# A recommendation tower on one core: wide triple products, a last chunk contracted by units, GpSimd with gathers only

## The reference: what is computed

```python
x_i = einsum('bmd,bhd->bmhd', X, prev_x).reshape(b, m * h, d)
x_i = einsum('oc,bcd->bod', W, x_i) + b[None, :, None]     # 128 outputs
cin_outs.append(x_i.sum(axis=2))                            # summed over d
```

## Time and profile before

| | us |
|---|---|
| three runs | 258.37, 261.34, 262.34 |
| median | 261.34 |
| the profiled execution | 258.26 |
| its span, first to last instruction | 256.5 |
| busy: TensorE / weight loads / VectorE | 209.3 / 173.8 / 127.2 |
| busy: ScalarE / GpSimd | 84.4 / 148.8 |
| mean granted TensorE clock (1 is full speed) | 0.939 |
| product matmuls L212, 4,096 records | 63.7 |
| contraction matmuls L371, 616 records | 76.9 |

### The profile page before, as it was taken

How to read it: one execution, slowest core, us unless ns; L and a number is a source line. 1 busy time by engine, 2 the same in 40 slices (tenths; PEclk the granted TensorE clock), 3 DMA queues, 4 the chain that set the end, 5 groups by cost and what they waited for, 6 DMA issues and landing times.

```text
span 256.5 us, 10809 instructions
## 1 busy us (share of the span) xinstructions
PE 209.3 (82%) x5049; PEld 173.8 (68%) x5049; DVE 127.2 (50%) x194; ACT 84.4 (33%) x159; POOL 148.8 (58%) x142
## 2 busy tenths in 40 slices
PE   7897899499007889799898796979698896999995
PEld 6664667287006769688787584968697796899541
DVE  0559487666920866838649548173918641000000
ACT  2575447264202961413433313142313310100141
POOL 4778788877899778778778778777750000000000
PEclk9999799979856999999999999799889997999999
DMA  6811111112810111111111111111110000000000
GB/s 206 299 26 20 31 28 23 24 33 35 279 22 3 23 26 25 30 23 31 30 24 30 27 24 31 20 32 28 29 26 3 5 3 5 0 3 0 0 0 0
DMA packets 6564, 9.66 MB, mean 38 GB/s; under 512 B 2804, under 2 KB 3256, under 8 KB 6520
## 3 DMA queue, kind: packets, MB, share of 16 engines
q0 software_dynamic: 4096, 4.20, 9.1%
q1 hardware_dynamic: 2136, 4.19, 4.7%
q10 hardware_dynamic: 288, 0.59, 0.7%
HBM read 8.97 MB, written 0.00 MB: 35 GB/s over the span
## 4 chain that ended last, share of the span: by engine, by line
POOL 43%; PE 36%; issue 15%; DMA 3%; ACT 2%; DVE 0%; DVEq 0%; ACTq 0%; POOLq 0%
POOL rows L413 39%; PE psum L371 19%; PE psum L212 7%; PE psum L491 3%; PE psum L482 3%; DMA rows<-table,idx 2%; POOL t_sb L306 2%; POOL prod L261 2%; PE psum L280 1%; PE psum L193 1%; PE psum L286 1%; ACT t_sb L229 1%; DMA t_sb<-ids 1%; PE psum L474 0%; ACT prod L250 0%
## 5 line engine op out<-in xcount | busy, mean ns | idle before, releaser
L413 POOL DMA_INDIRECT rows<-table,idx x128 | 138.8, 1085 | 40.6 <-issue 38.1
L212 PE MATMUL psum<-prod,xx 64*32 64x77 f32 x4096 | 63.7, 243 | 23.7 <-POOL prod L261 13.4
L261 DVE TENSOR_TENSOR prod<-xx 128x1024 f32<-128x1024 f32 x62 | 73.7, 1220 | 6.8 <-ACT xx L241 4.0
L212 PEld LDWEIGHTS psum<-prod,xx 64*32 64x32 f32 x4096 | 51.4, 109 | 35.9 <-issue 16.2
L371 PE MATMUL psum<-t_sb,coef 128*128 128x128 f32 x552 | 67.9, 285 | 2.1 <-issue 2.1
L371 PEld LDWEIGHTS psum<-t_sb,coef 128*128 128x128 f32 x552 | 66.7, 202 | 2.4 <-issue 2.2
L229 ACT ACTIVATE t_sb<-psum 128x616 f32<-128x616 f32 x34 | 23.3, 685 | 79.8 <-PE psum L212 79.8
L226 DVE COPY t_sb<-psum 128x616 f32<-128x616 f32 x30 | 23.9, 798 | 49.8 <-PE psum L212 49.6
L292 ACT ACTIVATE t_sb<-psum 128x276 f32<-128x276 f32 x32 | 20.7, 647 | 18.2 <-PE psum L280 18.0
L241 ACT ACTIVATE xx<-psum 128x512 f32<-128x512 f32 x32 | 17.5, 595 | 24.2 <-PE psum L193 24.2
L280 PE MATMUL psum<-w0p_sb,w_sb 128*128 128x276 f32 x64 | 21.8, 423 | 1.2 <-DVE w0p_sb L592 0.6
(11 more groups left out here) (33 smaller groups left out, 99.9 us busy)
## 6 DMA issues: line engine op xcount, KB each, us to landing
rows<-table,idx POOLq DMA_INDIRECT x128
w_sb<-w1t SPq DMA_DIRECT2D x3, 512.0 KB, 7.0
w_sb<-top SPq DMA_DIRECT2D x2, 512.0 KB, 5.3
t_sb<-w0x ACTq DMA_DIRECT2D x1, 512.0 KB, 4.8
w0x_sb<-w0g SPq DMA_DIRECT2D x1, 512.0 KB, 3.8
w_sb<-w1t SPq DMA_DIRECT2D x1, 384.0 KB, 5.6
t_sb<-w0p SPq DMA_DIRECT2D x1, 276.0 KB, 5.0
w_sb<-w1t SPq DMA_DIRECT2D x1, 128.0 KB, 4.8
```

What stands on the lines that cost most here:

```text
L212: last = pe.matmul(bank(TG + 2 * (v % 2) + r, n * COLS, COLS, 32 * (2 * e + k), M), xx[s % 2][D * r:D * (r + 1), x:x + M], prod[2 * (s % 2 ...
L261: last = dve.tensor_tensor(at(p, e * COLS, [[2 * COLS, SUB], [HALF, SHIFTS], [1, HALF]]), at(x, x0, [[M, SUB], [0, SHIFTS], [1, HALF]]), a ...
L413: pool.indirect_dma_start(rows[:, c:c + D], None, table[:, :], bass.IndirectOffsetOnAxis(ap=idx[:, g:g + 1], axis=0))\
```

## The change

Four edits, in one go:

1. A product matmul takes the two neighbouring classes of one element in one go, 154 columns. The four column groups hold two elements and two halves of `X`. The result of a group therefore lies otherwise in PSUM, and `copy_t` moves it in pieces of 64 partitions x 308 elements: four a group, all by ScalarE for even v, two by ScalarE and two by VectorE for odd v (all by ScalarE in unit 3). The ids are ordered anew to match.
2. The contraction of the chunk before is cut into 15 pieces, one behind each product group but the first of a chunk.
3. In the last chunk each unit's contraction runs during the step of the unit after (`unit_cin`): the unit's 32 columns of `t_sb` are stationary, the coefficients move, and four column groups of the array take every fourth term, in two PSUM banks by turns. VectorE copies the four partial sums out, a matmul with a stacked identity adds and transposes them (`sum_z`), ScalarE copies the result. Units of the last chunk are transposed one step before their products instead of two, behind product group v = 3, and their `xx`, Gram columns and pair products are made then.
4. GpSimd only gathers; the whole fold and all pair products are VectorE's, the fold's second part in four steps that release the coefficient transposes one by one.

```diff
         def t_group(pe, q, s, v):
...
-            for n in range(GROUP // 2):
-                j = (v % 2) * GROUP // 2 + n
-                for k in range(2):
-                    for e in range(2):
+            for n in range(2):
+                for p in range(2):
+                    j = 4 * (v % 2) + 2 * p + n
+                    x, y = (SUB // 2 * g + j) * 2 * M + HALF, 4 * j * COLS
+                    for k in range(2):
                         for r in range(2):
-                            last = pe.matmul(bank(TG + 2 * (v % 2) + r, n * COLS, COLS, 32 * (2 * e + k), M),
+                            last = pe.matmul(bank(TG + 2 * (v % 2) + r, 2 * n * COLS, 2 * COLS, 32 * (2 * p + k), M),
...
+        def copier(group, p):
+            return int(p == 1 and group % 2 == 1 and group // 4 != UNITS - 1)
...
-            src = at(psum, (TG + 2 * (v % 2)) * BANK, [[1, COLS], [BANK, 2], [COLS, GROUP // 2]])
-            dst = at(t_sb, t_at + s * UNIT + v * GROUP // 2, [[CHUNK, COLS], [SUB, 2], [1, GROUP // 2]])
-            copy(dst, src).then_inc(t_copied[v % 2], 1)
+            for p in range(2):
+                if copier(4 * u + v, p) != n:
+                    continue
...
+                for e in range(2):
+                    src = at(psum, (TG + 2 * (v % 2)) * BANK + e * COLS, [[1, COLS], [BANK, 2], [2 * COLS, 2]], D * p, D)
+                    dst = at(t_sb, t_at + s * UNIT + v * GROUP + 4 * p, [[CHUNK, COLS], [2, 2], [1, 2]], D * e, D)
+                    last = copy(dst, src)
+                last.then_inc(t_copied[n], 1)
...
+        def unit_cin(pe, s, part):
+            if part == 0:
+                for n in range(2):
+                    pe.wait_ge(t_copied[n], copied(n, 4 * (FIRST + s + 1)))
+                wait(pe, z_copied, s - 1)
+                for i in range(GRAM):
+                    unit_tile(pe, s, i % 4, 0, PAIRS + i, w0g_sb[:, i * O:(i + 1) * O], i < 4, i >= GRAM - 4)
+            for i in range(VCOLS * part // 4, VCOLS * (part + 1) // 4):
+                last = unit_tile(pe, s, i % 4, 1, i if i < PAIRS else COLS - 1, coef[:, i * O:(i + 1) * O],
+                                 i < 4, i >= VCOLS - 4)
+            if part == 3:
+                last.then_inc(unit_done, 1)
+
+        def unit_tile(pe, s, j, n, col, w, start, stop):
+            c = LAST_T + col * CHUNK + s * UNIT
+            return pe.matmul(bank(UNIT_ACC[s % 2], n * O, O, UNIT * j, UNIT), t_sb[:, c:c + UNIT], w,
+                             start=start, stop=stop, tile_position=(0, UNIT * j))
+
+        def copy_acc(dve, s):
+            dve.wait_ge(unit_done, s + 1)
+            wait(dve, z_done, s - 1)
+            dve.tensor_copy(acc_sb[s % 2][:, :], bank(UNIT_ACC[s % 2], 0, 2 * O)).then_inc(acc_copied, 1)
+
+        def sum_z(pe, s):
+            if s == 0:
+                pe.wait_ge(stack_ready, 1)
+            pe.wait_ge(acc_copied, s + 1)
+            for n in range(2):
+                last = pe.matmul(bank(UNIT_ACC[s % 2], 2 * O + n * UNIT, UNIT), acc_sb[s % 2][:, n * O:(n + 1) * O],
+                                 stack[:, 0:UNIT], start=True, stop=True)
+            last.then_inc(z_done, 1)
...
         @block.gpsimd
-                    if g == FOLD_AT:
-                        products(pool, 0, 3, 1, 0)
-                        products(pool, 0, 3, 1, 1).then_inc(pool_prod, 1)
-                        pool.wait_ge(u_pairs, M)
-                        pool.wait_ge(u_cross, M)
-                        fold_first(pool, POOL_SHIFTS, pool_step)
-                        pool.wait_ge(pool_step, 1)
-                        fold_second(pool, POOL_SHIFTS, pool_step)
...
         @block.tensor, step
                 for v in range(4):
                     t_group(pe, q, s, v)
-                if ahead[2]:
+                    if v == 3 and ahead[1] and late(ahead[1]):
+                        transpose_rows(pe, *ahead[1])
+                    if s + v > 0:
+                        cin(pe, q - 1, last_at, 4 * s + v - 1, 4 * UNITS - 1)
+                    if q == CHUNKS - 1 and s > 0:
+                        unit_cin(pe, s - 1, v)
+                        if s > 1 and v == 2:
+                            sum_z(pe, s - 2)
+                if ahead[2] and not late(ahead[2]):
                     transpose_rows(pe, *ahead[2])
-                cin(pe, q - 1, last_at, s)
...
             for j in range(TOP1 // 128):
+                if L1 + j not in UNIT_ACC:
+                    l1_dense(pe, j)
             for part in range(4):
-                cin(pe, c, c % 2 * COLS * CHUNK, part)
+                unit_cin(pe, UNITS - 1, part)
+                if part == 1:
+                    sum_z(pe, UNITS - 2)
+            for j in range(TOP1 // 128):
+                if L1 + j in UNIT_ACC:
+                    pe.wait_ge(z_copied, UNITS - 1)
+                    l1_dense(pe, j)
+            sum_z(pe, UNITS - 1)
+            pe.wait_ge(acc_free, 2 * CHUNKS - 2)
+            pe.wait_ge(z_copied, UNITS)
...
         @block.scalar, step
                     act_copy_t(act, q, t_at, s, 2 * g)
-                    if ahead[1]:
+                    act_copy_t(act, q, t_at, s, 2 * g + 1)
+                    if ahead[1] and not late(ahead[1]):
                         act_gram(act, *ahead[1], g)
...
+                if ahead[1] and late(ahead[1]):
+                    for g in range(2):
+                        act_xx(act, *ahead[1], g)
+                        act_gram(act, *ahead[1], g)
...
         @block.vector
-            fold_first(dve, DVE_SHIFTS, fold_step)
+            fold_first(dve, range(2 * SHIFTS), fold_step)
             dve.wait_ge(fold_step, 1)
-            fold_second(dve, (0, SHIFTS), fold_step)
-            fold_second(dve, [s for s in DVE_SHIFTS if s % SHIFTS], fold_step)
+            for i in range(SHIFTS):
+                fold_second(dve, (i, SHIFTS + i), fold_step)
```

More of the change, by code:

```diff
@@ L76, in build @@
         ident = sb("ident", 128)
+        stack = sb("stack", 3 * UNIT)
+        acc_sb = [sb(f"acc_sb{n}", 2 * O) for n in range(2)]
         cin_bias = sb("cin_bias", 4)
@@ L181, in _, with copied @@
             sp.wait_ge(stored, 16)
+        def copier(group, p):
+            return int(p == 1 and group % 2 == 1 and group // 4 != UNITS - 1)
+        def copied(n, groups):
+            return sum(copier(i, p) == n for i in range(groups) for p in range(2))
         def transpose_rows(pe, q, s):
@@ L333, in transpose_coef @@
         def transpose_coef(pe, n):
[L334 to L338 removed]
+            if n < HALF and n % 4 == 0:
+                pe.wait_ge(fold_step, 2 + n // 4)
             if n >= 4:
@@ L369, in cin @@
                     pe.wait_ge(coef_ready[n], COPIER.count(n))
-            for n, w, wc, tc, first, end in CIN[len(CIN) * part // 4:len(CIN) * (part + 1) // 4]:
-                last = pe.matmul(bank(n, 0, CHUNK), w[:, wc:wc + O], t_sb[:, t_at + tc:t_at + tc + CHUNK],
+            for n, w, wc, tc, first, end in CIN[len(CIN) * part // parts:len(CIN) * (part + 1) // parts]:
+                last = pe.matmul(bank(ACC, n * CHUNK, CHUNK), w[:, wc:wc + O], t_sb[:, t_at + tc:t_at + tc + CHUNK],
                                  start=first, stop=end)
-                if end:
-                    last.then_inc(cin1_done if n == ACC + 1 else t_free, 1)
+            if part == parts - 1:
+                last.then_inc(t_free, 1)
@@ L382, in chunk, with late @@
+        def late(unit):
+            return unit[0] == CHUNKS - 1
         def chunk(step, q, final=False):
@@ L449, in _ @@
                 if n == C_BANKS.index(TG):
-                    pe.wait_ge(t_copied[0], UNITS * 2)
+                    for p in range(2):
+                        pe.wait_ge(t_copied[p], copied(p, UNITS * 4 - 1))
                 transpose_coef(pe, n)
@@ L656, in _ @@
                 chunk(lambda q, s, ahead: step(q, s, ahead, q % 2 * COLS * CHUNK), c, final=c == CHUNKS - 1)
+            for s in range(UNITS - 2, UNITS):
+                copy_acc(dve, s)
             dve.wait_ge(l3_done, 1)
```

159 lines of the change are left out of this document (77 added, 82 removed).

## The result

| | before | after |
|---|---|---|
| median of four runs | 259.86 | 246.5 |
| all four | 257.95 to 262.34 | 244.96 to 247.44 |
| ratio, 95% interval | | 0.950 [0.940, 0.961] |
| profiled execution / its span | 258.26 / 256.5 | 246.13 / 244.3 |
| TensorE granted clock, mean | 0.939 | 0.965 |

The account below looks back on a forecast made before the run. GpSimd's gathers were taken to bound the kernel to 156 us, TensorE afterwards. Of the 20 us gain, 9 came from gathers and 11 from unit-wise contraction; 235.1 plus 1.6 clock and 1.8 around the span gave 238.5, said as 239, range 229 to 250.

Parts of the forecast that it names:

- The rows: Gathered rows on GpSimd: closing a 9.2 us hole in the gathers lets TensorE start unit 11's transposes at 138.9 us.
- Cover: Before unit 11's transposes TensorE would be ready at 135.4, rows at 138.9; the first 3.5 us of error cost nothing.
- The price of transposing late: Last chunk: 4.15 us from a unit's transposes to its first product group, with TensorE waiting for copies and products.
- Dense tail: Dense layers after the last contraction: unchanged at 17.8 us.
- the 1.6 that I had allowed: Allowance in the sum for one stretch of TensorE matmuls at the lower clock behind a new wait, 1.6 us.
- the clock rival: Each of four late waits loses 1.6 to 1.7 us to the lower clock: 244, or 247 with lengthened waits; chance 0.12.
- my main case: The forecast case: 234 to 244 us for the whole kernel; chance 0.50.
- the stalls: TensorE's stalls inside product groups stay, 1.25 us for each of the five last steps: 245 us; chance 0.10.
- the dear copies: Evacuation copies of half the partitions cost as much as whole ones, 0.69 us each on ScalarE: 245 us; chance 0.08.
- the change of shape: Switching matmul shape on TensorE between products and contraction pieces: 0.1 us each, making a 10-record piece 1.25 us.
- the slow rival: Unit contraction: column groups do not overlap while 32-column weights load, 0.113 us a record, 288 us; chance 0.05.

Follow-up runs that it names:

- the hole put back: Changed kernel with five additions into an unused buffer on GpSimd before gather 50, delaying rows from unit 6 on; 257.9 us, ratio 0.987.
- the merged kernel: Changed kernel with the contraction pieces of the chunk before and of units put two by two behind product groups 1 and 3; 238.3 us, ratio 0.928.
- edit 4 alone: Kernel before with only the pair products and whole fold moved to VectorE, so GpSimd only gathers; 251.5 us, ratio 0.971.
- narrow ones in the changed kernel: Changed kernel with each product matmul of 154 columns split into two of 77; 256.3 us, ratio 0.981.
- without units but with early transposes: Changed kernel, last chunk contracted in one go at the end, transposes of units 12 to 15 behind product group 1, not 3; 238.6 us, ratio 0.925.

## Why the prediction was right, and where its steps were wrong

**Right.** The rows set the start of the late chain: unit 11 at 139.7 for 138.9, and the hole put back comes out at the end. That the start came within 0.8 is in part luck: in the four other kernels without an edit before that point unit 11 starts between 137.1 and 141.2, by how long the gathers of that execution took. Cover: the coefficient stage and the longer ScalarE work of the first units cost nothing, with more slack than I had. The price of transposing late, 4.15 us to the next product group, was 4.35 to 4.6. Dense tail: 17.8 without the clock.

**The sum of +7.6 us in the span**, by its terms: 0.8 the rows; 0.4 the rest of steps 10 and 11; 1.7 step 12, in which two groups took 2.10 and ten records 2.17 us at the lower clock; 0.9, 1.2 and 1.3 the steps 13, 14 and 15; 1.0 unit 15's contraction and the last sums; 1.8 the first dense layer at the lower clock, 8.80 instead of 7.03; less the 1.6 that I had allowed for one such stretch. Two stretches came where I counted one, and only one of them behind a late wait, so the clock rival is half true: 244 us, its low end, is nearer to the 246 measured than my main case. The rivals of the stalls and of the dear copies, priced at 245, are as near by number only: from unit 11 on no product group stalls in its middle, and the copies cost 0.42 us, not 0.69.

**The step that was mis-sized** is the change of shape in the late steps, 0.1 for what is 0.16 to 0.34. In the sum it stands in the pieces. A piece of 10 contraction records takes 1.31 us and not 1.25, a unit's pieces 1.65 and 1.21 and not 1.5 and 1.1; a product group, its own change included, took the 0.7 that I gave it. Of the 3.4 us of steps 13 to 15 the pieces are 2.3 (0.4 of it because two pieces have 12 records), 1.0 is the price of the late transposes and 0.3 the sums over column groups, 0.56 each and not 0.4; the groups give 0.2 back. The rule of the Trainium skill that I set beside it (TensorEngine Tiling, Key Properties: a change of tiling mode drains TensorE) speaks of such changes, and the merged kernel, with fewer of them, agrees with it: 0.7 us less for a round of three.

The records of a unit's contraction were nearly right, 70 in 2.10 us, 0.030 each against 0.028. The column groups overlap, so the slow rival is out. The ratio of the Trainium skill for column tiles (TensorE: Matmul & The Clock Gate, Measured speedup vs the span model), by which I had estimated 5.5 us a unit, comes near to the 5.3 measured in pieces, but by changes of shape: in runs of 84 and 70 records a unit takes 4.6.

**The attribution was wrong.** I wrote that 9 us come from the gathers and 11 from contracting the last chunk by units, and gave the wide matmuls nothing but vanished stalls. My own sum did not say so. It charges the units 11.1 us in steps 13 to 15, 1.1 behind them, 4.45 at the end and 1.6 for the sums over column groups, 18.3 us, where the contraction in one go takes 17.4. What it takes out lies in the steps: from unit 11's transposes to the dense start the kernel before needs 72.2 us, with stalls and three stretches at the lower clock, and my sum without the unit pieces and sums 57.9.

Measured one by one: gathers 7.3 (edit 4 alone, of which 2.2 are seen as earlier rows), wide matmuls 9.8 (narrow ones in the changed kernel, some 6 if the late rows of that run are left out), contraction by units minus 4.3: 9 to 13 of the 13.4. These are differences from two different kernels, and edit 2 and the late transposes were not tried from the kernel before, so that they add up proves little. I had argued from equal streamed columns that a group would keep its 0.7 us. But 0.7 was the cost of a wide group; narrow ones between contraction pieces take 0.84 to 1.05. Twice the matmuls, each with its own weight load, over equal columns: that the number holds them is my reading, and which part of a matmul does it is not shown.

**Best version.** The changed kernel with merged pieces, 238.3, and without units but with early transposes, 238.6, are equal within their intervals. Both keep edits 1 and 4.

**Open.** Whether the slower gathers of some runs (1.09 to 1.14 us each) have a cause in the kernel; whether the early transposes help the merged kernel with units, which was not tried; when a wait is followed by the lower clock and when not.

## What to carry to other kernels

Cutting a long contraction into pieces to fill waits pays only where there is a wait: count on the critical engine what each piece adds, its changes of matmul shape too (0.16 to 0.34 us each here), and put as few pieces as cover the wait. Small matmuls on array tiles can cost by their number although the streamed columns are equal, here 0.84 to 1.05 us against 0.68 a group; try fewer and wider ones. When several edits go in together, time each alone before explaining the sum: here one of them cost some 4 us inside a gain of 13. And run the kernel that you compare with in the same set.

## What I had not expected of the hardware

- TensorE's clock fell behind a stretch of 3 us in which the profile shows it busy throughout (221 to 224) and a wait of only 0.65 us; in three of five traces with these matmuls and this wait, and in two not.
- The same program took 1.38 times as long in one set, 357 us against 259 in another set under the same chip number, with TensorE's matmuls in bursts of 3 to 7 and no releaser.
- A waiting step can cost twice: 2.68 us of wait, and 1.6 to 1.9 us more for the contraction behind it at 1.2 GHz; behind other waits of 2.45 to 2.79 us that loss did not come.
